# Products of zeros on TensorE in the first attention's lead and behind the last made stack

## What is computed

```
x = x + L0_attn_a(layernorm(x))     # 16 heads of 16, 4 key heads, rotation, mask by blocks of 128
x = x + L0_ffn(layernorm(x))        # 64 experts, top 8
x = x + L0_attn_b(layernorm(x))     # window of 128 and 4 sinks
x = x + L0_ffn(layernorm(x))
x = x + L1_attn_a(layernorm(x))     # 16 key heads, everything seen
x = x + L1_ffn(layernorm(x))
x = x + L1_attn_b(layernorm(x))     # latent attention
x = x + L1_ffn(layernorm(x))
```

## Time and profile before

| | us |
|---|---|
| three runs | 1902.12, 1904.87, 1903.46 |
| median | 1903.46 |
| the profiled execution, its own time | 1902.33 |
| its span, first to last instruction | 1900.5 |
| PE busy in the span | 1805.4 (95%) |
| mean granted PE clock | 0.986 |

### The profile page before, as it was taken

How to read it: one execution, slowest core, us unless ns; L and a number is a source line. 1 busy time by engine, 2 the same in 40 slices (tenths; PEclk the granted TensorE clock), 3 DMA queues, 4 the chain that set the end, 5 groups by cost and what they waited for, 6 DMA issues and landing times. The chain is left out here.

```text
span 1900.5 us, 30194 instructions
## 1 busy us (share of the span) xinstructions
PE 1805.4 (95%) x10580; PEld 1240.3 (65%) x10580; DVE 1071.4 (56%) x1854; ACT 912.9 (48%) x1938; POOL 695.1 (37%) x627
## 2 busy tenths in 40 slices
PE   6899999999999899999999999799999999999998
PEld 3333688888887555788888886433335677777776
DVE  6776444444445664544444446788865666555544
ACT  3677533333333565433333333478874456445431
POOL 5200466666665110456666664500001344221200
PEclk8899999999999999999999999999999999999999
DMA  4400344444440320353344440590001000000000
GB/s 127 122 1 1 93 113 116 113 115 112 112 106 7 92 76 2 98 142 104 101 111 116 116 119 0 119 171 1 1 1 23 1 1 1 1 1 1 1 12 12
DMA packets 137931, 121.77 MB, mean 64 GB/s; under 512 B 84545, under 2 KB 122905, under 8 KB 137593
## 3 DMA queue, kind: packets, MB, share of 16 engines
q1 hardware_dynamic: 137817, 120.24, 25.4%
HBM read 111.41 MB, written 8.65 MB: 63 GB/s over the span
## 5 line engine op out<-in xcount | busy, mean ns | idle before, releaser
L1418 DVE TENSOR_TENSOR e_inner_lo<-e_inner,e_inner_hi 128x512 fp32r<-128x512 f32 x192 | 243.9, 1270 | 380.3 <-ACT e_inner_hi L1381 380.1
L1404 POOL TENSOR_TENSOR e_wsilu<-e_silu,e_rw 128x512 f32<-128x512 f32 x192 | 262.1, 1365 | 204.7 <-ACT e_silu L1375 180.6
L1351 PE MATMUL psum<-e_x_hi,e_w_hi 128*128 128x512 f32 x768 | 302.8, 394 | 4.8 <-DVE e_inner L1426 4.8
L1351 PE MATMUL psum<-e_x_lo,e_w_hi 128*128 128x512 f32 x768 | 299.6, 390 | 0.0
L1351 PE MATMUL psum<-e_x_hi,e_w_lo 128*128 128x512 f32 x768 | 299.0, 389 | 0.0
L1375 ACT ACTIVATE e_silu<-psum 128x512 f32<-128x512 f32 x192 | 114.8, 598 | 343.0 <-PE psum L1351 343.0
L1413 POOL TENSOR_TENSOR e_w_lo<-e_raw,e_w_hi 128x384 fp32r<-128x384 f32 x180 | 221.2, 1230 | 133.6 <-ACT e_w_hi L1392 121.9
L1351 PEld LDWEIGHTS psum<-e_x_hi,e_w_hi 128*128 128x128 f32 x768 | 144.1, 188 | 45.5 <-DVE e_inner L1426 15.8
L1088 DVE TENSOR_REDUCE c_mx<-psum 128x1 f32<-128x1024 f32 x128 | 150.6, 1219 | 26.5 <-PE psum L957 26.0
L1351 PEld LDWEIGHTS psum<-e_x_hi,e_w_lo 128*128 128x128 f32 x768 | 144.2, 188 | 30.7
L1351 PEld LDWEIGHTS psum<-e_x_lo,e_w_hi 128*128 128x128 f32 x768 | 144.2, 188 | 29.0
(11 more groups left out here) (356 smaller groups left out, 3175.0 us busy)
## 6 DMA issues: line engine op xcount, KB each, us to landing
e_rw<-e_rw_dram SPq DMA_DIRECT2D x56, 384.0 KB, 5.2
e_rw<-e_rw_dram SPq DMA_DIRECT2D x56, 256.0 KB, 5.4
e_raw<-in_L_ffn_w_gate SPq DMA_DIRECT2D x64, 192.0 KB, 2.6
e_raw<-in_L_ffn_w_up SPq DMA_DIRECT2D x64, 192.0 KB, 2.6
e_raw<-in_L_ffn_w_down SPq DMA_DIRECT2D x32, 384.0 KB, 3.5
e_rw<-e_rw_dram SPq DMA_DIRECT2D x72, 128.0 KB, 4.7
e_rw<-e_rw_dram SPq DMA_DIRECT2D x16, 192.0 KB, 3.0
c_parts_dram<-c_part SPq DMA_DIRECT2D x8, 384.0 KB, 2.5
```

What stands on the lines that cost most here:

```text
L1351: last = nc.tensor.matmul(bank[u % 2][:], self.w[a][s][:, KC * which + k, j * P:(j + 1) * P], self.x[b][:, k, h * HALF:(h + 1) * HALF], st ...
L1404: self.core.nc.gpsimd.tensor_tensor(self.wsilu[:, u % 2, :], self.silu[:, u % 2, :], self.rw[s][:, j, h * HALF:(h + 1) * HALF], ALU.mult). ...
L1418: self.core.nc.vector.tensor_tensor(self.inner_parts[1][:, u % 3, :], self.inner[:, u % 2, :], self.inner_parts[0][:, u % 3, :], ALU.subtr ...
```

## The change

A helper `zeros(count)` issues products of `zero_h` (128x128 stationary, 512 columns moving) into bank 3; nobody reads them, and no instruction waits for them. There are 63: 53 in the lead of attention a and its first maxima, 10 behind the last made stack of attention c.

```diff
-        for n in range(3):
-            self.a.turn(pe, n)
+        def zeros(count):
+
+            for _ in range(count):
+                core.nc.tensor.matmul(core.bank[3][:], core.zero_h[:, 0:P], core.zero_h[:], start=True, stop=True)
+
+        self.a.turn(pe, 0)
+        self.a.turn(pe, 1)
+        pe.wait_ge(core.ones_made, 2)
+        pe.wait_ge(self.a.copied, TT)
+        pe.wait_ge(self.a.v_copied, TT)
+        zeros(4)
+        self.a.turn(pe, 2)
+        zeros(4)
         for n in range(5):
             self.made.make(pe, self.a, n)
+            zeros({2: 1, 4: 2}.get(n, 0))
         pe.wait_ge(start.const_made, 1)
 
         def ahead(what, p, *more):
+            if (what, p, *more) == ("rows", 0, 0):
+                zeros(10)
             if what == "max" and p == 0:
                 n = QUART * more[0] + more[1]
+                zeros(2)
                 if n in (2, 3):
                     self.a.turn(pe, n + 1)
                 if n == 7:
@@ -2427,6 +2442,8 @@
         c.turn(pe, 7)
         for n in range(10, 12):
             self.made.make(pe, c, n)
+        pe.wait_ge(c.copied, TT)
+        zeros(10)
```

## The result

The changed kernel took a median of 1896.07 us over 7 runs (1890.77 to 1897.59), the kernel before, run in turns with it, 1902.83 us over 7 (1901.77 to 1904.87). The ratio is 0.9961 with a 95% interval of [0.9951, 0.9971]: 6.8 us at the medians, 5.5 to 9.3 by the interval. The forecast was 1899.4 us with a range of 1896.2 to 1902.4.

What follows compares the result with a forecast made beforehand. PE, busy 95% of the span, was taken as the bound, so the change could pay only through its clock. +0.3 - 3.9 - 0.5 = -4.1 us from 1902.33 gave 1898.2, plus 1.1 for the median: 1899.4 us, range 1896.2 to 1902.4.

Steps and rivals of the forecast that it cites:

- The later phases unchanged: Phases after the lead's first stage of rows: the profile would show them unchanged, only 3.6 us sooner.
- the barrier: Barrier before `Second`: ten products delay it 0.3 us, 0.8 us gained behind it; net -0.5 us, ends -1.4 and +0.5.
- The stage behind the rows: Lead, first rows to block 2's exponentials: full clock gives -3.9 us, between -3.0 and -4.5, with ACT next in line.
- The eleven around the turn and the stacks: Lead: eight around the third turn cost nothing; made stacks up to 0.9 us earlier, bank 7 opened at 35.1 us.
- The maxima: Lead's 16 maxima with 32 zero products: last read at 47.15 us against 47.04, +0.1 us at their end.
- Rival 1: Zeros pace PE in the maxima, the ten delay rows (+1.3), stage gains only 3.0: 1901.7 us, chance 0.20.
- The ten in front of the rows: Before the lead's first rows: ten products take 2.16 us against 1.83 us of idleness, +0.2 us.
- Rival 3: Clock outlives the barrier (-0.9 more), stage gives its full 4.5, shift meets less of POOL's work: 1897 us, chance 0.13.
- Rival 2: Zeros don't hold the clock, which falls at 39.9 us in the lead's maxima as before: 1910 us, chance 0.05.
- Rival 4: Every half-clock stretch in the lead and around the barrier shrinks by half, giving 15 us: 1888 us, chance 0.02.

Runs made afterwards that it cites:

- the one with six zeros: Changed kernel with POOL's split of the first expert weights held until the third shift is ready, six instead of ten products before the first rows: 1895.26 us, ratio 0.9955.
- the held one: Changed kernel with POOL's split of the first expert weights waiting until the third shift is ready: 1891.04 us, ratio 0.9945; timed again 1894.0 us, ratio 0.9965.
- the run with 34 more: Changed kernel with POOL's split held behind the third shift, plus 34 zero products at other places where the clock still fell: 1892.72 us, ratio 0.9945.

## Why the forecast was too small

Two steps of it failed, and together they are more than the miss. "The later phases unchanged" put at nothing a piece that came out 2.7 us shorter. And the barrier was put at a gain of 0.8 us behind it, where 2.1 were measured. The terms in order:

**The stage behind the rows: right in size.** -3.9 forecast, -4.0 measured, and 9.5 us in every profile in which the zeros kept the clock (in six others 11.6 to 13.5 us). The exponentials of block 0 to those of block 2 took 57.95 - 53.24 = 4.7 us where 4.6 had been read from the later twins. Only the next bound was named wrongly: in that stretch ACT waited for PE twice, 1.0 us in all, and PE was busy for 9.36 of the stage's 9.54 us, so it is PE at full clock and not ACT.

**The eleven around the turn and the stacks: right in size, by the luck of the execution.** 0.7 us to bank 7 against 0.9 forecast, and the eleven alone gain nothing (1.0001), as forecast. But in two of the five profiles without them the piece took 5.2 us too. The forecast took a fall that one execution showed for a property of the kernel.

**The maxima: a term mis-sized.** The shift was begun 0.5 us later relative to the first made stack than before, where +0.1 was forecast; with 13.07 us busy of 13.78 PE had next to no slack, which was Rival 1's mechanism: it has the rows at +1.3 us, the forecast at +0.3, and they came at +0.7 behind the first made stack.

**The ten in front of the rows: mis-sized, and their part in the gain not seen.** The forecast put them at +0.2 us, with a shift that would be ready at the same time. The shift took only 1.6 us from 48.20 us, where it had taken 2.0 before, so the first row waited 0.76 us for the zeros; it came at 50.54 us, past the 50.5 that the forecast named as a sign against it (0.6 of that is the late start). In the sum they stand as a pure cost. That doesn't make the sum wrong, since its -3.9 assumes a clock that is held, but the forecast never says that it is these ten that hold it there. In the one profile in which only these ten are missing the clock falls in the very stage that pays, 13.2 us instead of 9.5, and the kernel is 3.0 us slower at the medians. They cost 0.7 us at the first row and carry 3.7 in the stage.

**"The later phases unchanged but 3.6 us sooner": the first step that failed.** Between the second and the fourth phase the executions differ by 2.7 us, 1.4 of it the third shift beside POOL's split and the rest the fall of the clock behind it. This is the sentence of Rival 3 on a shift that meets less of POOL's work; at the first shift it came true as well (1.6 us for 2.0), but there the ten zeros swallowed it. It doesn't follow from the zeros alone: one profile of the changed kernel has the collision, one hasn't. What is shown is that the collision costs (holding POOL alone: 2.4 us at the medians, ratio 0.999 [0.9981, 0.9999], just clear of nothing, and pooled 2.7 us on top of the change). How much of that is the longer shift and how much the fall is less sure: all eight profiles with the collision have a fall there, and of the seven without it one has, the one with six zeros. Whether the change makes the collision rarer isn't shown: of the nine profiles without the hold only one escaped it, the changed kernel's first. Some 2 us more hang on a fall near 200 us, at the start of the expert block, which is missing in six profiles, five of which are among the seven with no collision; in the changed kernel's first profile it is there.

**The barrier: right in form, mis-sized, the second step that failed.** The barrier came 0.25 us later (0.3 forecast). Behind it c's rows came 2.07 us sooner, where -0.8 was taken and -1.7 was the best end: the clock outlived the barrier in each of the eight profiles with the ten, and fell in each of the six without them and in that with the narrow ones. So half of Rival 3 was the case. Of the 2.07, 0.9 are given back at once in this profile (the fall at 1225.60 us lasts 10.3 us, where before it lasted 6.8); of the eight with the ten three have this longer fall, the other five don't and reach the next phase in 22.1 us or less, where the kernel before took 22.3. What the ten are worth to the whole kernel isn't settled: by the ratios 0.8 us on the kernel before and 2.3 on the changed and the held one, with intervals that overlap each time, and against the pooled means only 1.2 and 1.4.

**The sum** of the trace's terms is +0.6 - 0.7 + 1.5 - 4.0 - 2.7 - 0.5 - 2.1 + 1.7 = -6.2 us, which is the difference of the spans. Against the forecast of -4.1 that is 2.1 too much: -2.7 for the phases that were to stay unchanged, -1.3 for c's first maxima and -0.8 between the fourth phase and `Second` (the expert block among it), against +0.6 for the start, +0.4 for the first row and +1.7 for the end, of which 0.9 is the longer fall; a second fall in that piece, at 1447 us, lasts 6.8 us, where the one at the same place lasted 3.4 before. The largest is the piece with the collision. The times of all runs, some of them with the collision, have a mean gain of 6.1, so the profiled execution is no outlier; how it splits into these terms is known for this one execution only. The range was too narrow because each of the two mechanisms stood in a rival of 0.13 that demanded "every term at its better end". (In Rival 1 the words have the barrier lose 0.1 us; its sum of -1.8 counts it as gained.)

**Rivals.** Rival 2 (zeros don't hold the clock) is refuted: 1.00 throughout the lead in the changed kernel, and with the narrow ones it fell. Rival 4, all of the half clock back, comes out both wrong and right. Across kernels it is wrong: the run with 34 more had 0.997 of the clock as the mean of its runs against 0.994 of the 12 held ones, about 12 us less at half clock, and was 1.3 us faster. Within one kernel it holds: over the 19 runs of the changed kernel the listed clock and the time go together; four of the six values:

| granted clock | runs | mean us |
|---|---|---|
| 0.991 | 3 | 1900.5 |
| 0.993 | 3 | 1897.9 |
| 0.994 | 6 | 1895.1 |
| 0.996 | 3 | 1891.1 |

Each 0.001 of the mean clock is 0.001 x 1895 / 0.5 = 3.8 us at half clock, and by a straight line through all 19 it costs 1.9 us, half of its length. The Trainium skill (TensorE: Matmul & The Clock Gate, Terms) puts the penalty at about the throttled time times (1 - K/N), which is that half; for the falls that come and go from one execution of the changed kernel to the next these runs agree, though falls and the collision come together and the line can't part them. From the kernel before to the changed one it doesn't hold: 0.008 of clock, 30 us at half clock, went for 6.8 us. Part of it lay under DVE's maxima, where PE wasn't the bound, and 63 products of zeros had to be worked off; how the rest divides between these two wasn't measured.

## What to carry to other kernels

Time at half clock is worth taking back only where TensorE itself is the bound: find the stretch where its busy time fills the window at 0.50, and put wide products of nothing into the idleness *in front of* that stretch, the last wait before it above all; those that look like pure delay there may be the ones that carry the gain. Test such a filler by its narrow twin, which has all the same waits and a sixteenth of the work. And before a gain of some microseconds is booked, profile the same program twice: an execution is one sample of which falls and which collisions happen, and a collision seen in one of them can be ordered away by a single wait, worth 2 to 3 us here.

## What had not been expected of the hardware

- Four DVE operations on 128x16 took 2.2 us while POOL worked on 128x384 operands, 0.8 us otherwise: 0.65 against 0.18 us for the first, 0.85 against 0.19 for the last, and each slow one ended within 0.05 us of the end of an operation of POOL's.
- Products with both operands of zeros kept the clock at 1.00 through the lead when they were 512 columns wide; 32 columns wide, at the same 63 places, they let it fall at 42.1 us.
- The clock fell behind a wait of only 1.46 us (without the ten) and of 1.77 us (third shift), and not behind 2.86 us at the barrier with 2.11 us of full products ahead of it and the next maxima right behind. At the third phase it fell in one held execution and not in another, with PE busy for 1.94 of 2.90 us in front of it in both: the wait and the work in front of it didn't decide it alone.
- The places of the falls differ from execution to execution of one kernel, and with them its time: 1890.8 to 1901.5 us in 19 runs of the changed kernel. POOL could begin on the same load 3.5, 3.9 and 5.6 us after its issue in three profiles; why isn't settled.
